# Window attention with its queries and keys sent a pair further ahead: first steps reordered, MLP weights loaded later, zero products on TensorE

## The reference, cut to what matters

```python
xn = _layer_norm(x, norm1_g, norm1_b)
xw = windows(roll(xn, (-4, -4)))                 # 64 windows of 64 tokens
q, k, v = split(xw @ qkv_w.T + qkv_b)            # 16 heads of 8 channels
q, k = _rope2d(q), _rope2d(k)
attn = softmax(q @ k.T * 8 ** -0.5 + attn_mask)  # 64 x 64 for each head and window
x = x + roll(unwindow((attn @ v) @ proj_w.T + proj_b), (4, 4))
x = x + mlp(_layer_norm(x, norm2_g, norm2_b))    # fc1, silu gate, fc2
```

## Time and profile before

| | |
|---|---|
| median of 3 runs | 406.61 us (405.34 to 406.91) |
| the profiled execution, its own time | 399.32 us |
| its span, first to last instruction | 397.5 us |
| TensorE products busy | 351.2 us (88%) |
| VectorE busy | 301.9 us (76%) |
| ScalarE busy | 271.4 us (68%) |
| GpSimd busy | 270.9 us (68%) |
| mean granted TensorE clock | 0.986 |

### The profile page before, as it was taken

The page is one execution under the profiler, slowest core; times in us unless marked ns, Lnnn a source line. Parts: engine busy times, 40 slices in busy tenths (PEclk is TensorE's granted clock), DMA queues, the critical chain, the costliest instruction groups (busy, mean ns, idle before and its releaser), DMA issues.

```text
span 397.5 us, 12541 instructions
## 1 busy us (share of the span) xinstructions
PE 351.2 (88%) x4900; PEld 228.8 (58%) x4900; DVE 301.9 (76%) x830; ACT 271.4 (68%) x435; POOL 270.9 (68%) x322
## 2 busy tenths in 40 slices
PE   2668999998999999998979899999998989989693
PEld 0335665565555666666656456654674856657373
DVE  6758888887888888889677677787668797784424
ACT  3466888886877788887835644455478877868481
POOL 7477966667777777798776786756257785868421
PEclk9999999999999999999899999999999999999799
DMA  5701100111111000010000000000010011010102
GB/s 181 253 20 28 30 24 22 27 28 30 27 31 31 26 26 26 26 30 15 2 3 2 15 13 2 2 2 0 2 29 14 15 51 31 2 55 2 53 2 58
DMA packets 15597, 12.29 MB, mean 31 GB/s; under 512 B 3992, under 2 KB 14137, under 8 KB 15545
## 3 DMA queue, kind: packets, MB, share of 16 engines
q1 hardware_dynamic: 14208, 11.03, 9.5%
q10 hardware_dynamic: 1336, 0.54, 0.5%
HBM read 4.22 MB, written 2.10 MB: 16 GB/s over the span
## 4 chain that ended last, share of the span: by engine, by line
PE 61%; DVE 16%; ACT 6%; issue 5%; DMA 5%; SPq 3%; POOL 2%; ACTq 0%; DVEq 0%; POOLq 0%
PE ps L359 8%; PE ps L1577 7%; PE ps L911 6%; PE ps L939 5%; PE ps L993 4%; PE ps L932 4%; DMA k_t<-qk_t 4%; PE ps L920 3%; PE ps L901 3%; SPq L871 3%; PE ps L379 3%; DVE ob L1701 2%; PE ps L903 2%; DVE mx L1670 2%; PE ps L1419 2%
## 5 line engine op out<-in xcount | busy, mean ns | idle before, releaser
L1752 POOL TENSOR_TENSOR el<-e,eh 128x1024 f16<-128x1024 f32 x28 | 59.6, 2131 | 31.1 <-ACT eh L1744 30.8
L1297 POOL TENSOR_TENSOR p_lo<-e_buf,p_hi 128x1024 f16<-128x1024 f32 x32 | 68.2, 2130 | 5.6 <-ACT p_hi L1153 3.8
L1289 POOL TENSOR_TENSOR rot<-ta,tb 128x256 f32<-128x256 f32 x32 | 23.3, 728 | 39.1 <-DVE tb L1084 38.3
L359 PE MATMUL ps<-y_t,fc_w 128*128 128x512 f16 x192 | 46.2, 380 | 2.8 <-DVE y_t L582 1.2
L1111 DVE TENSOR_REDUCE ps<-ps 128x16 f32<-128x1024 f32 x32 | 39.4, 1232 | 8.0 <-PE ps L920 7.2
L911 PE MATMUL ps<-mask,identb 128*128 128x512 bf16 x128 | 39.9, 394 | 6.4 <-DMA k_t<-qk_t 6.2
L1735 ACT ACTIVATE e<-ps 128x1024 f32<-128x1024 f32 x32 | 32.6, 1020 | 18.5 <-PE ps L1566 18.1
L1577 PE MATMUL ps<-val,eh 128*128 128x129 f16 x512 | 38.6, 226 | 7.5 <-DVE ob L1701 6.9
L1223 ACT ACTIVATE e_buf<-ps 128x1024 f32<-128x1024 f32 x32 | 32.7, 1023 | 15.6 <-PE ps L932 15.4
L1577 PEld LDWEIGHTS ps<-val,eh 128*128 128x128 f16 x512 | 32.5, 100 | 18.4 <-issue 11.0
L288 POOL TENSOR_TENSOR hl<-hid,hh 128x512 f16<-128x512 f32 x24 | 27.7, 1159 | 19.7 <-DVE yn L569 10.5
(11 more groups left out here) (164 smaller groups left out, 986.4 us busy)
## 6 DMA issues: line engine op xcount, KB each, us to landing
k_t<-qk_t SPq DMA_DIRECT2D x126, 32.0 KB, 1.9
x_all<-in_x SPq DMA_DIRECT2D x8, 256.0 KB, 4.5
out<-ob SPq DMA_DIRECT2D x8, 192.0 KB, 2.1
yr<-xr SPq DMA_DIRECT2D x16, 64.0 KB, 2.0
mask_f<-in_mask SPq DMA_DIRECT2D x1, 512.0 KB, 3.6
fc_w<-in_fc_w SPq DMA_DIRECT2D x1, 512.0 KB, 5.4
out<-ob SPq DMA_DIRECT2D x4, 128.0 KB, 1.9
fc_w<-in_fc_w SPq DMA_DIRECT2D x1, 256.0 KB, 5.3
```

The lines of the kernel that those rows point to most:

```text
L359: last = pe.matmul(ps[:, bank, :], fc1_w16[:, ws, 128 * block_:128 * block_ + 128], y_t[:, v, ys, :], start=(n == 0), stop=(n == 2))
L1297: pool.tensor_tensor(p_lo[:, u], e_buf[:, u], p_hi[:, u], ALU.subtract).then_inc(plo_done, 1)
L1752: pool.tensor_tensor(el[:, T % H_BUFS, :], e4[:, T % E_BUFS, :], eh[:, T % H_BUFS, :], ALU.subtract).then_inc(el_done, 1)
```

## The change

- Steps start at -3. Projection, rope and rows are those of pair n+3, the turn, the copy to `qk_t` and the key transfers those of pair n+2. `qk_t` gets four buffers instead of two, and each of the four key buffers a semaphore of its own.
- In steps 0 to 2 (`early`) the scores and the maximum stand ahead of the projection and the rotation of rows on TensorE and VectorE; ScalarE's and the turn's places follow.
- Statistics of chunks 4 to 7 move to the ends of steps 2, 4, 6 and 8; GpSimd's norm chains follow them. Those of chunks 2 and 3 on GpSimd stand behind the low rows of pair 2.
- ScalarE normalises chunk 2 after the exponential's place in step 0 and chunk 3 in step 1, both with the projection weights behind them; the scaling of `fc1_w` moves from step 0 to step 3.
- The nine loads of `REST` are issued in step 0, between the keys of pair 1 and of pair 2.
- TensorE multiplies a tile of zeros, 128 x 512, 15, 9, 7, 5 and 3 times (39 products) at places where it waited, into bank T2.

```diff
+                    if at_step(n, 0):
+                        for dst, name in REST:
+                            sp.dma_start(dst[:], t[name]).then_inc(rest_loaded, 16)
+                    if valid(n, -2):
+                        sp.wait_ge(qt_ready, n + 3)
...
-                        for j in range(2 if at_step(n, -1) else 4):
+                        for j in range(2 if at_step(n, -2) else 4):
                             rows = slice(ROWS * j, ROWS * j + ROWS)
-                            sp.dma_start(k_t[rows, (r + 1) % BUFS, j], qk_t[rows, (r + 1) % 2, 1]).then_inc(kz_ready[(r + 1) % 2], 16)
+                            sp.dma_start(k_t[rows, k, j], qk_t[rows, k, 1]).then_inc(kz_ready[k], 16)
...
+                def keep_busy(count):
+                    for k in range(count):
+                        pe.matmul(ps[:, T2_BANK, :], zeros[:, 0:128], zeros[:], start=True, stop=True)
+                pe.wait_ge(zeros_set, 1)
+                keep_busy(15)
...
                 ln_turn(0)
+                keep_busy(9)
...
+                    def rows_turned():
+                        if at_step(n, -2):
+                            keep_busy(7)
+                        if at_step(n, -1):
+                            keep_busy(5)
+                        if valid(n, -2):
+                            wait(pe, lo_done, n + 3)
+                            wait(pe, qt_ready, n + 2)
...
+                            turn(t1_ps[:, 0], q_rows[:, (r + 2) % BUFS])
+                            turn(t1_ps[:, 1], k_rows[:, u]).then_inc(t1_done, 1)
+                    if not early(n):
+                        rows_projected()
+                        rows_turned()
                     if valid(n, 0):
                         if at_step(n, 0):
+                            keep_busy(3)
                             pe.wait_ge(mask_lo if parts > 1 else mask_hi, 1)
-                        pe.wait_ge(kz_ready[u], it * 64 + 64)
+                        pe.wait_ge(kz_ready[r], it * 64 + 64)
...
+                    if early(n):
+                        rows_projected()
...
-                    if at_step(n, 0) or at_step(n, 1):
-                        ln_stats_of(4 + 2 * n)
-                        ln_stats_of(5 + 2 * n)
+                    if early(n):
+                        rows_rotated()
...
+                    if stats_chunk(n):
+                        ln_stats_of(stats_chunk(n))
```

More of the change, by code:

```diff
@@ L114, in build @@
         warm2 = sb("warm2", [128, 1])
+        zeros = sb("zeros", [128, CHUNK], F16)
+        zeros_set = sem("zeros_set")
         until_mlp = ExitStack()
@@ L184, in build @@
         qt_ready = sem("qt_ready")
-        kz_ready = [sem(f"kz_ready{u}") for u in range(2)]
+        kz_ready = [sem(f"kz_ready{k}") for k in range(BUFS)]
         s_done = sem("s_done")
@@ L818, in ln_chunk, with stats_chunk @@
                 return LN_STEP.get(n - first) if isinstance(n, int) else None
+            def stats_chunk(n):
+                return n // 2 + 3 if isinstance(n, int) and n in range(2, 2 * CHUNKS - 6, 2) else None
             def nothing(left):
@@ L839, in steps, with early @@
                 other_steps(eng, body, mlp_early)
+            def early(n):
+                return isinstance(n, int) and 0 <= n < 3
             def at_step(n, step):
@@ L857, in _ @@
                         sp.dma_start(mask_f[:], t["mask"]).then_inc(mask_loaded, 16)
-                for dst, name in REST:
-                    sp.dma_start(dst[:], t[name]).then_inc(rest_loaded, 16)
                 sp.wait_ge(keys_set, 1)
@@ L946, in body @@
                     v = 1 - u
-                    if valid(n, -2):
-                        wait(pe, rope_done, n + 2)
-                        pe.wait_ge(ln_ready, (n + 2) // TPC + 1 if isinstance(n, int) and n < LOOP_FROM else CHUNKS)
-                        project(qkv_ps[:, 0:2 * DIM], n + 2, slice(0, 2 * DIM)).then_inc(qk_done, 1)
-                    if at_step(n, -2):
-                        pe.wait_ge(mask_top, 1)
-                        pe.matmul(ps[0:1, T1_BANK, 0:1], mask_max[:], ln_const[:, 2, 0:1], start=True,
-                                  stop=True).then_inc(mask_summed, 1)
@@ L1077, in body @@
                     v = 1 - u
-                    if valid(n, -2):
-                        dve.wait_ge(qk_done, n + 3)
-                        wait(dve, r_done, n + 1)
-                        x = qkv_ps[:, 0:2 * DIM].rearrange("p (a h d) -> p a h d", a=2, h=HEADS)
-                        for dst, k in ((ta, 0), (tb, 1)):
-                            last = dve.tensor_tensor(dst[:, u], x,
-                                                     rope[:, k].unsqueeze(2).broadcast_to([128, 2, HEADS, HD]), ALU.mult)
-                        last.then_inc(rope_done, 1)
@@ L1228, in body @@
                         copy(q_t2[:, u], t2_ps).then_inc(q2_ready, 1)
+                    if early(n):
+                        rows_high()
+                    if at_step(n, 1):
+                        ln_norm_of(3)
+                        act.wait_ge(attn_loaded, 16 * len(ATTN))
+                        act.activation(proj_ws[:], proj_w[:], ACT.Copy, scale=WSCALE).then_inc(proj_w_scaled, 1)
+                        act.wait_ge(proj_w_scaled, 1)
+                        copy(proj_w16[:, 0, :], proj_ws[:]).then_inc(proj_w_hi, 1)
                     if valid(n, 1):
```

155 lines of the change are left out of this document (88 added, 67 removed).

## The result

The changed kernel takes 406.38 us in the median of 20 runs (402.79 to 408.95), the kernel before 403.86 in the median of 20 runs beside them. The ratio is 1.0078, with an interval of 1.0054 to 1.0101: **0.8% slower**, where 403.5 and a gain of 3.1 us were forecast. The time lies inside the range (399.8 to 407.0), but the sign is wrong. That the time came so near was luck: the error of 2.9 us is smaller than the error of the difference, because the three runs shown ahead (406.61) lay 2.75 above the longer series.

The account below looks back on a forecast made before the run. The prediction took TensorE to set the loop's pace, with slow key landings reaching it, and GpSimd, ScalarE and VectorE the start. Sum: -2.9 - 0.7 + 0 + 0.5 + 0 = -3.1, so 406.6 becomes 403.5; range 399.8 to 407.0.

Parts of the forecast that it names:

- Keys a pair further ahead: Loop, pairs 12 to 30: key transfers sent a step earlier no longer delay TensorE, 18 steps fall to 85.86 us, -2.9 us.
- Rival 4: Loop: VectorE's chain replaces the key wait, most of 4.93 us a step stays, about 406.5 us; chance 0.09.
- The end: Last steps: pair 31's 0.69 us wait for its keys goes, the MLP's first piece follows on its own chain, -0.7 us.
- The start: Up to pair 3's scores: the path through GpSimd, ScalarE and VectorE starts them near 40.6 instead of 40.10, +0.5 us.
- Rival 2: Start: the clock level falls back (1.6 us) or pair 2's keys come late (1 us), 405.3 us; chance 0.17.
- Pairs 3 to 12: These nine steps: no change, ScalarE's order kept and the MLP weights' scaling put in step 3, 0, bounds -1 and +1.
- MLP loads: Start: nine issues behind pair 1's keys delay pair 2's, covered because the maximum waits for VectorE anyway, 0.
- Zero products: Start: 15 fill the wait before 6.84 and end near 7.3, 0.5 late; the clock level rises during them.
- rival 3: Start: the zero products don't lift the level and stand in the way, +6.3 us, 409.8 us; chance 0.07.
- Rival 1: Start: the 4 us by which pair 1's scores come early survive, -7.1 us in all, 399.5 us; chance 0.12.

Follow-up runs that it names:

- r1_before: The kernel before, unchanged, run and profiled a second time: 406.79 us.
- f1: The changed kernel with 26 more zero products in TensorE's waits at the start and nothing else: 403.59 us, ratio 1.0027 to the kernel before.
- e6: The changed kernel with five moves at its start (pair 0's high values, MLP scaling, statistics, a norm chain, low exponentials, all earlier): 403.45 us, ratio 0.9935.
- e1: The changed kernel with VectorE's statistics of chunks 4 and 5 in step -1, those of 6 and 7 at the end of step 1: 405.85 us.
- e5: The changed kernel with only ScalarE's scaling of fc1_w moved from step 3 to the end of step 2: 406.37 us, ratio 1.0052.
- e8: e7 with the nine MLP loads behind pair 3's keys and the scaling of the MLP weights at the end of step 11: 399.98 us, ratio 0.9950.
- e2: The changed kernel without any of the 39 zero products: 407.9 us, ratio 1.0212 to the kernel before.
- e7: e6 with 21 more zero products in TensorE's waits at the start: 399.66 us, ratio 0.9910 to the kernel before.
- e11: e8 with half the MLP bias scaled on ScalarE and the sixteen one-column bias products ahead of pair 31's scores: 397.14 us, ratio 0.9845.
- r3_before: The kernel before, unchanged, run and profiled a third time: 399.52 us.
- f2: The changed kernel with the scaling of half the MLP bias on ScalarE instead of VectorE and nothing else: 406.63 us, ratio 1.0080.

## Why the prediction was wrong in sign

**Keys a pair further ahead, -2.9: right.** A step of the loop takes 85.9/18 = 4.77 us in the changed kernel, TensorE waits for no keys between pairs 12 and 30, and -2.7 was measured. Rival 4 (VectorE takes over) falls.

**The end, -0.7: right in size, but its cover was missed.** Pair 31's scores do follow 0.7 sooner. The step says that the MLP's first piece follows "on its own chain", and takes the 0.7 us at full value. That chain runs through VectorE, where the MLP's statistics (L548) stand ahead of pair 31's maximum. The chain that ended last in the changed kernel, at this place (start, length, what):

```profile
183.36 0.88 DVE stats L548 x4
...
185.16 1.24 DVE ps L1160
...
187.37 3.02 PE ps L522 x16
```

VectorE's timeline of the kernel before:

```profile
182.38 0.87 DVE L546 BATCH_NORM_STATS2 stats<-x 128x6 f32<-128x128 f32 x4
...
184.18 1.23 DVE L1111 TENSOR_REDUCE ps<-ps 128x16 f32<-128x1024 f32 x1
```

The statistics start 183.36 - 178.77 = 4.59 us after pair 30's scores and the maximum 6.39; in the profile of before 4.60 and 6.40 behind 177.78. So the earlier scores only wait for VectorE. At equal length of the low level (6.8 us) the entry takes 16.45 in `r1_before` and 17.1 in the changed kernel: the 0.7 is given back within 15 us. The other 1.2 of the entry's +1.8 goes with the level. With 3.4 us at the low level it takes 14.7 in two profiles of before, with 6.8 it takes 16.5 to 17.2. Nothing in the forecast's sum stood for that.

**The start, +0.5: the waits right, the clock left out.** The chain was worked out to 0.3 us, and `f1`, at the full level, starts pair 3 at 40.61. What failed is "I let the level rise" as a state that stays. Rival 2 named the place (pair 2's scores, the turn for pair 5) and the mechanism, and is what came there. Its price of one third of a step, 1.6 us, was too low: it was 2.5 up to pair 3 and 0.9 in steps 3 and 4, and at 0.17 its chance was too. The earlier fall near 22 us, in two of three profiles, no rival named. The Trainium skill (TensorE: Matmul & The Clock Gate, section HAM oscillation) says that a wait between bursts of products brings the clock down. The trace agrees in part. All three profiles have the fall 0.4 us into the wait of 2.94 us, so that wait alone doesn't bring it; in the first, TensorE was busy 4.79 of the 7.40 us before. In two profiles an earlier fall follows a wait of about 2 us, while the first (1.94) and `e6` (2.16) have such a wait and no fall behind it. So `f1` shows that filled waits keep the level, but which wait brings it down is open.

**Pairs 3 to 12, "0", from ScalarE having room in step 3: wrong.** +1.9: 0.9 goes with the level (`f1`), and 1.0 is left at the full level. `e6` takes as much away (50.19 to 49.14), 0.6 in step 3 (5.67 to 5.09) and 0.5 in step 5 (6.53 to 6.03), where pieces were moved away; that the new pieces in steps 2 to 8 make the 1.0 is argued from this and from `e1`. The step looked for a free engine, but these steps take turns between three: `e1` and `e5` show that with one cover gone the next ends last. VectorE's statistics are rows of 0.87 us each ahead of a copy that TensorE waits for (changed kernel, VectorE):

```profile
37.12 0.86 DVE L1071 BATCH_NORM_STATS2 stats<-x_all 128x6 f32<-128x128 f32 x4
...
63.21 0.87 DVE L1071 BATCH_NORM_STATS2 stats<-x_all 128x6 f32<-128x128 f32 x4
...
65.20 0.68 DVE L1142 COPY qk_t<-ps 128x1024 f16<-128x1024 f16 x1
```

And in TensorE's timeline of the changed kernel the turn that stands behind it:

```profile
66.00 0.63 PE L892 MATMUL ps<-ident,xn 128*128 128x128 f32 x4 [0.89 <-DVE qk_t L1142]
```

**MLP loads, 0: right.** The nine issues took 5.1 us, 0.7 more than worked out, and pair 2's keys came late (mask at 31.14 after 1.62 us of waiting, worked out 30.5). Each of the four key transfers landed 1.8 to 2.1 us after its issue, so the bytes ahead of them in the queue added little. `e8` shows 0.4 us of the delay at pair 3. That this wait has a part in the fall of the level is possible; no run moves the loads in the changed kernel itself.

**Zero products:** they end near 7.3 as forecast, and rival 3 falls with `e2`: without them pair 0 comes 1.0 later and the median is 1.5 higher. Rival 1 falls too; pair 1's early scores (25.39, worked out 24.5) bring nothing.

**Open:** what brings the level down at the start, how the remaining +0.15, a mean of stretches from 199.6 to 205.6, splits, and what `e7`'s zeros save beyond the start. At the entry, why the low level lasts 3.4 us in two profiles of before and 6.8 in the third, and 6.8 in all three of the change, is open too; `e11` shows only that it goes when the bias products stand elsewhere.

## What to carry to other kernels

Ask of waits on TensorE not only how long they are but whether the level survives them: here a start with waits of 1.6 to 2.9 us between short bursts cost 3.4 us more by the low level, and products of zeros in the waits gave that back. Before work is moved into a busy step, see which engine ends last there and which comes next once that one is relieved. And a gain in a last step is worth nothing until the chain that starts the next stage has been followed engine by engine.

## What was not expected of the hardware

- The spread of runs goes with the granted clock. In the kernel before a span of 397.5 us goes with 0.989 and one of 406.3 with 0.963, and the same instructions behind pair 31's scores took 214.3 us in `r3_before` and 222.0 in `r1_before`.
- TensorE can be busy by its row and still be at the low level. At the entry of the changed kernel it shows 6.80 of 6.80 us at 0.50. The stretch begins at 187.6, 0.4 us into sixteen one-column products that follow a wait of 1.20 us and take 3.19 there, 1.90 in `e11`.
- A small scaling on VectorE takes ten times its time beside GpSimd. In `r3_before` it starts just ahead of GpSimd's `p_lo` (189.50); in VectorE's timeline:

```profile
189.46 0.17 DVE L670 TENSOR_SCALAR fc_bias<-fc_bias 128x4 f32<-128x4 f32 x1
```

In `e7` it starts 0.50 us behind GpSimd's `p_lo` (185.01, 2.26 long) and ends with it:

```profile
185.51 1.78 DVE L672 TENSOR_SCALAR fc_bias<-fc_bias 128x4 f32<-128x4 f32 x1
```

The Trainium skill (SBUF — State Buffer, section Who interferes with whom) says that such an instruction, where it runs in a mode that uses two ports, and one of GpSimd lock a shared pair of ports from each other, and that the one issued second waits until the first is through. The trace agrees: 0.17 us when it starts first, 1.78 us, to GpSimd's end, when it starts second. It cost nothing here (`f2`).
